# Splitting weight blocks on other engines: GpSimd's work in two grouped attentions handed to ScalarE and VectorE

## The reference

```python
# B: 32 query heads, 8 key heads, head width 128, 16 sequences of 64 tokens
q = (query @ Wq).reshape(nb, q_len, H, D).transpose(0, 2, 1, 3)
k = (key @ Wk).reshape(nb, q_len, KVH, D).transpose(0, 2, 1, 3)
v = (value @ Wv).reshape(nb, q_len, KVH, D).transpose(0, 2, 1, 3)
q = q * cos + _rotate_half(q) * sin
k = k * cos + _rotate_half(k) * sin
...
scores = jnp.where(mask == 0, -1e9, q @ k.T / sqrt(D))
x = softmax(scores) @ v          # k, v repeated for the 4 heads of a group
return x.reshape(nb, q_len, H * D) @ Wo
# D: the same without cos and sin, causal, query = key = value source
```

## Time and profile before

| | |
|---|---|
| time, median of 3 runs | 1838.44 us (1837.08 to 1838.74) |
| profiled execution, first to last instruction | 1832.8 us |
| PE busy | 1679.7 us, 92% |
| DVE busy | 1065.0 us, 58% |
| ACT busy | 603.0 us, 33% |
| POOL busy | 525.5 us, 29% |
| stretch of B's four passes of `turn` | 321.8 to 938.5 us |
| stretch of D's four passes of `turn` | 1037.9 to 1583.6 us |

### The profile page before, as it was taken

One profiled execution on the slowest core, in us unless ns is written; L12 is line 12 of the kernel. 1 busy time (PEld: TensorE's weight loads), 2 busy tenths in 40 slices (PEclk: granted clock), 3 DMA queues, 4 the chain that ended last, 5 costly groups with the idle time before them and its releaser, 6 DMA issues. The chain is left out here.

```text
span 1832.8 us, 24019 instructions
## 1 busy us (share of the span) xinstructions
PE 1679.7 (92%) x8910; PEld 1336.7 (73%) x8910; DVE 1065.0 (58%) x2105; ACT 603.0 (33%) x1199; POOL 525.5 (29%) x297
## 2 busy tenths in 40 slices
PE   8897879889998988989888999999999999888998
PEld 6665658667776866777677777777877877676866
DVE  3878775766676577566754245355265245517645
ACT  2564533223322323232243222222222222425541
POOL 4316123330323052120133323233053031432330
PEclk9998999899998989999999999999999999999999
DMA  4002011110111020000010111011021010112231
GB/s 178 14 18 81 25 35 46 47 35 12 36 35 46 1 70 24 23 24 24 23 42 27 57 35 47 12 57 46 0 69 46 0 46 24 47 33 61 71 91 46
DMA packets 26173, 75.78 MB, mean 41 GB/s; under 512 B 3904, under 2 KB 4640, under 8 KB 25824
## 3 DMA queue, kind: packets, MB, share of 16 engines
q1 hardware_dynamic: 25696, 73.42, 12.4%
q0 software_dynamic: 384, 1.05, 0.2%
HBM read 72.36 MB, written 2.10 MB: 41 GB/s over the span
## 5 line engine op out<-in xcount | busy, mean ns | idle before, releaser
L83 PE MATMUL bankA<-sb_xT,sb_Bwq 128*128 128x512 f32 x768 | 196.7, 407 | 0.0
L83 PE MATMUL bankY<-sb_Bwo,sb_BoT 128*128 128x512 f32 x768 | 195.9, 405 | 0.2 <-DVE sb_BoT L978 0.2
L83 PE MATMUL bankY<-sb_Dwo,sb_DoT 128*128 128x512 f32 x768 | 192.3, 399 | 2.0 <-POOL sb_Dwo L694 1.8
L83 PE MATMUL bankA<-sb_xT,sb_Dwq 128*128 128x512 f32 x768 | 189.9, 396 | 0.0
L83 PEld LDWEIGHTS bankY<-sb_Bwo,sb_BoT 128*128 128x128 f32 x768 | 142.8, 192 | 44.2 <-issue 15.0
L83 PEld LDWEIGHTS bankA<-sb_xT,sb_Bwq 128*128 128x128 f32 x768 | 147.4, 195 | 36.0 <-issue 2.7
L83 PEld LDWEIGHTS bankY<-sb_Dwo,sb_DoT 128*128 128x128 f32 x768 | 139.8, 188 | 44.0 <-issue 10.9
L83 PEld LDWEIGHTS bankA<-sb_xT,sb_Dwq 128*128 128x128 f32 x768 | 142.3, 188 | 33.9 <-issue 2.7
L919 DVE TENSOR_TENSOR sb_BqT<-bankA,sb_Btable 128x512 f32<-128x512 f32 x64 | 44.3, 692 | 183.5 <-ACT sb_Bsw L842 183.5
L78 POOL TENSOR_TENSOR sb_Bwo<-sb_raw,sb_zero 128x1024 fp32r<-128x1024 f32 x16 | 31.3, 1955 | 372.9 <-PE bankY L83 364.3
L78 POOL TENSOR_TENSOR sb_Dwo<-sb_raw,sb_zero 128x1024 fp32r<-128x1024 f32 x16 | 31.6, 1973 | 335.1 <-PE bankY L83 335.1
(11 more groups left out here) (253 smaller groups left out, 3406.3 us busy)
## 6 DMA issues: line engine op xcount, KB each, us to landing
sb_raw<-in_w_attn SPq DMA_DIRECT2D x80, 512.0 KB, 3.5
sb_raw<-in_q_gu SPq DMA_DIRECT2D x22, 256.0 KB, 2.7
sb_raw<-in_q_d SPq DMA_DIRECT2D x11, 256.0 KB, 2.6
sb_rawx<-in_xT SPq DMA_DIRECT2D x4, 512.0 KB, 8.0
sb_raw<-in_wqk SPq DMA_DIRECT2D x8, 256.0 KB, 2.6
sb_xtok<-in_x_tok SPq DMA_DIRECT2D x1, 2048.0 KB, 12.7
sb_raw<-in_ctxT SPq DMA_DIRECT2D x4, 512.0 KB, 3.8
sb_raw<-in_ctx_tok SPq DMA_DIRECT2D x4, 512.0 KB, 3.8
```

The costliest lines, as they stand in the source:

```text
L83: last = nc.tensor.matmul(out, lhs, rhs, start=start and i == 0, stop=stop and i == len(pairs) - 1)
```

## The change

All blocks of the passes of `turn`, 36 in each attention, are split elsewhere. The high part becomes a copy with ACT into the float32r buffer, the low part the same subtraction on DVE. POOL keeps the four blocks of `start` and the clearing of `kt`. The conditions for overwriting a buffer go along to ACT. In a `turn` the blocks have places in the slots: o0 and o2 in slots 0 and 8, on ACT ahead of `pt`, on DVE ahead of rotation, `front` and `back`; o1 and o3 in the same slots, on ACT after `pt`, on DVE after the low part of `oT`; the others at the end of the slot that `SPLIT_AT` names, on DVE after the low part of `oT` and ahead of a late `front`.

```diff
+    SPLIT_AT = {1: "q0", 3: "q1", 4: "k", 6: "v", 9: "q2", 11: "q3"}
...
                 @block.gpsimd
                 def _(pool):
-                    def split(part):
-                        for n, name in enumerate(part.blocks):
-                            if part.order is not START:
-                                if name == "o0":
-                                    pool.wait_ge(wo_used, part.it * 2 + 1)
...
-                            pool.wait_ge(w_raw[n % 2], (part.weights + n - n % 2) * 8 + 16)
-                            high_part(dst[name][0], raw[n % 2][:]).then_inc(w_high, 1)
-                            pool.wait_ge(w_high, part.weights + n + 1)
-                            nc.gpsimd.tensor_tensor(dst[name][1], raw[n % 2][:], f32(dst[name][0]), ALU.subtract).then_inc(w_low, 1)
-                            if part.order is START and name == "k":
-                                nc.gpsimd.memset(kt[:], 0.0).then_inc(padded, 1)
-                    run(pool, split, split)
+                    part = Part(first, START, START_BLOCKS)
+                    for n, name in enumerate(START_BLOCKS):
+                        pool.wait_ge(w_raw[n % 2], (part.weights + n - n % 2) * 8 + 16)
+                        high_part(dst[name][0], raw[n % 2][:]).then_inc(w_high, 1)
+                        pool.wait_ge(w_high, part.weights + n + 1)
+                        nc.gpsimd.tensor_tensor(dst[name][1], raw[n % 2][:], f32(dst[name][0]), ALU.subtract).then_inc(w_low, 1)
+                        if name == "k":
+                            nc.gpsimd.memset(kt[:], 0.0).then_inc(padded, 1)
...
+                    def weights_high(part, name):
+
+                        if name not in part.blocks:
+                            return
+                        n = part.blocks.index(name)
+                        if name in ("o0", "o2"):
+                            act.wait_ge(wo_used, part.it * 2 + (1 if name == "o0" else 2))
+                        elif name in ("o1", "o3"):
+                            act.wait_ge(y_done, part.it * SLOTS + (2 if name == "o1" else NT + 2))
+                        else:
+                            used = {"q0": ("Q", 5), "q1": ("Q", 7), "k": ("Q", 5), "v": ("Q", 5), "q2": ("Q", 13), "q3": ("Q", 15)}[name]
+                            act.wait_ge(a_ready, part.bank(used) + 1)
+                        act.wait_ge(w_raw[n % 2], (part.weights + n - n % 2) * 8 + 16)
+                        nc.scalar.activation(dst[name][0], raw[n % 2][:], ACT.Copy).then_inc(w_high, 1)
...
+                            if u % NT == 0:
+                                weights_high(part, "o2" if u else "o0")
                             act.wait_ge(t_ready, part.unit(u) + 1)
                             nc.scalar.activation(pt[u % 2][:], bankT[u % 2][:, 0:GROUP * S], ACT.Copy).then_inc(pt_done, 1)
+                            if u % NT == 0:
+                                weights_high(part, "o3" if u else "o1")
...
+                            if u in SPLIT_AT:
+                                weights_high(part, SPLIT_AT[u])
...
+                    def weights_low(part, name):
+
+                        if name not in part.blocks:
+                            return
+                        n = part.blocks.index(name)
+                        dve.wait_ge(w_high, part.weights + n + 1)
+                        nc.vector.tensor_tensor(dst[name][1], raw[n % 2][:], f32(dst[name][0]), ALU.subtract).then_inc(w_low, 1)
...
+                            if u % NT == 0:
+                                weights_low(part, "o2" if u else "o0")
                             in_turns(rotate(part, *banks) if rope and banks else None,
...
+                            if u % NT == 0:
+                                weights_low(part, "o3" if u else "o1")
+                            if u in SPLIT_AT:
+                                weights_low(part, SPLIT_AT[u])
                             if late(u):
                                 in_turns(scores)
```

## The result

The changed kernel takes 1766.84 us (median of 4 runs, 1765.95 to 1768.82) where the kernel before, run beside it, takes 1837.81 (1837.08 to 1838.74). The ratio is 0.9613, with a 95% interval of 0.9599 to 0.9626: 71 us faster. Forecast were 1764.5 us and a range of 1756 to 1788. The profiled execution took 1767.49 us beside a span of 1765.6, against 1832.8 of span before: 67.2 us of span.

What follows compares the result with a forecast made beforehand. In B's split slots, DVE instructions with two SBUF inputs stall beside POOL and PE waits. B gains 67.6 us (616.7 to 549.1), D 6.3, together 73.9: 1838.4 - 73.9 = 1764.5 us, range 1756 to 1788.

Steps and rivals of the forecast that it cites:

- the signs named: Profile afterwards: POOL empty in the turns, B's full passes 145 to 146 us at clock 1.00, D's 143 to 144.
- passes without the waits below: B's four passes: taken as D's 545.7 less its 7.4 us of waits, 538.3 us, products at full clock.
- rotation waits, twelve places: B's score products still wait for a rotation, 12 x 0.6 = 7.2 us of the earlier 23.4.
- slots 0 and 8, seven places: Splits of o0/o1 and o2/o3 in B, the tight place: 0.2 us booked for each of seven, 1.4 us.
- `pt` of the first slot: First slot of each attention: ACT's 1.06 us copy delays `pt(0)`, 1.1 us lost in B and 1.1 in D.
- waits for L978: Near the end of B, with no split there: 1.1 us of PE waits that stay.
- The clock: B's passes: granted clock returns to 1.00 as in D; otherwise 22.8 us would not come back, giving 1787.
- The first rival: Clock stays low in B because it keeps more waits than D: gain 51.1, time 1787 us; chance 0.06.
- The six other blocks: cost zero: q0 to q3, k, v at the ends of six slots: copy and low part covered, 1.4 us to spare.
- Low parts half exposed in B: Each of B's 36 blocks costs PE 0.6 us, 22 us go back: 1786 us; chance 0.11.
- The slower rival: Each block's copy and subtraction, 2.3 us, falls on PE's path: 1930 us; chance 0.03, with slower mixtures.
- No change: DVE's long instructions are not POOL's doing and the new work fits in idle time: 1838 us; chance 0.01.

Runs made afterwards that it cites:

- D alone: The change made in D only, B keeping its splits on POOL, against the kernel before: 1831.72 us, ratio 0.9963.
- the pair of useless loads: Changed kernel with POOL given two instructions per block on data nobody waits for: reading SBUF 1849.41 us, ratio 1.0054; only writing 1770.33, 0.9621.
- the rotation first: Changed kernel with late slots reordered: ACT's swap copies ahead of `pt`, DVE's rotation ahead of `back`; 1760.40 us, ratio 0.9583 to the kernel before.

## Why the prediction was right, and what was mis-sized

*What bounds the kernel, and by what.* Right, and shown: the waits of the earlier trace rows went with POOL's reads and came back with useless ones. The prices of the parts, 1.06 and 1.23, were measured as 1.06 and 1.22. Of the signs named, D's passes came a little better than 143 to 144 (142.5 to 143.4), and B's second and third, at 146.6 and 149.6, lie outside 145 to 146.

*B.* Here is the term that was off most. It said "B becomes 538.3 + 7.2 + 1.4 + 1.1 + 1.1 = 549.1", and it measured 554.6. Piece by piece:

| piece of B | booked | measured |
|---|---|---|
| passes without the waits below | 538.3 | 540.9 |
| rotation waits, twelve places | 7.2 | 7.0 |
| slots 0 and 8, seven places | 1.4 | 0 |
| `pt` of the first slot | 1.1 | 1.35 |
| waits for L978 (now L997) | 1.1 | 1.0 |
| waits behind the loop's jump | 0 | 4.3 |
| sum | 549.1 | 554.55 |

The waits are those of the list above, and for `pt` a single line of the order of time (below). The first row is D's passes without their wait for `pt` in the first slot, 537.9 - 0.8 = 537.1, and 3.8 us on top, by which PE is busy for longer in B's passes (534.9) than in D's (531.1). 3.3 of the 3.8 are in B's third pass: 145.79 against 142.5. This row isn't products at full clock alone, as the forecast had it: the 2.2 us of the last slot are in it in B and in D, before and after. The sum meets the 554.6 of the windows. Of the 5.5 us too many, 4.3 are the waits behind the jump. They were left out of the sum, though they were in the trace of before, 1.76 and 1.66 us at the same place. The sum took D's passes as its floor, and D's loop has no such wait.

*The clock.* "I let B's clock come back" was right for most of it: PE's busy time in B fell from 554.7 to 534.9, 19.8 of the 22.8 us. The first rival, a clock that stays low at 1787 us, is refuted: B's first two passes are at 1.00, with their rotation waits of 0.56 us. The third pass is not. The stretches behind the two loop jumps:

```profile
469.40:477.00 7.60, 5.44 (x31) 4.16 (x30) 5.63 (x12) 2.51 (x5) 0.00 (x0) 1.00 0.18 65
...
616.00:624.00 8.00, 5.88 (x21) 4.33 (x20) 5.96 (x12) 2.38 (x4) 0.00 (x0) 0.67 0.24 71
```

The same wait, 2.16 us at the second pass and 2.12 at the third, was followed by products at the full 2.4 GHz in the one and by a mean granted clock of 0.67 in the other, so part of that stretch ran at 1.2 GHz. The Trainium skill's rule on brief, frequent pauses ("TensorE: Matmul & The Clock Gate", section "A second HAM failure mode: psum-queue depth-cycling") isn't borne out by the pauses of 0.56 us here. What decides after one of 2.1 us these runs don't settle. Over the eleven profiles with the loop, the clock is below 1.00 in the 8 us behind 13 of the 22 waits, and length alone doesn't decide: it fell behind one of 1.94 us (B alone moved) and not behind one of 2.52 (low parts of o0 to o3 twice).

*D.* Booked 6.3, measured 7.8 in the windows and 7.9 for D alone. All waits on `back` and POOL went, and `pt(0)` cost this:

```profile
326.33 0.70 PE L791 MATMUL bankO<-sb_Bpt,sb_BV 64*128 64x256 f32 x4 [1.35 <-ACT sb_Bpt L879]
...
980.33 0.70 PE L791 MATMUL bankO<-sb_Dpt,sb_DV 64*128 64x256 f32 x4 [0.79 <-ACT sb_Dpt L879]
```

The 1.1 booked for each attention is the mean of the two, 1.35 in B and 0.79 in D. Before the change PE waited 0.41 us there in B, at 323.59, so the copy ahead of `pt(0)` added 0.94. D's passes without this wait came out 1.2 us below the floor of 538.3.

*The six other blocks: cost zero.* Right in the trace that was read. In a slot with q2:

```profile
543.26 0.42 ACT L842 ACTIVATE sb_Bsc<-sb_Bsc 128x256 f32<-128x256 f32 x1 [2.78 <-DVE sb_Bsc L948]
...
543.59 1.04 ACT L857 ACTIVATE sb_Bwq<-sb_raw 128x1024 fp32r<-128x1024 f32 x1
...
544.66 1.22 DVE L975 TENSOR_TENSOR sb_Bwq<-sb_raw,sb_Bwq 128x1024 fp32r<-128x1024 f32 x1 [0.50 <-ACT sb_Bwq L857]
...
547.39 0.69 DVE L928 TENSOR_TENSOR sb_BqT<-bankA,sb_Btable 128x512 f32<-128x512 f32 x1 [1.50 <-ACT sb_Bsw L830]
```

ACT does the copy behind its exponential, DVE the low part behind that, and DVE still stands idle for 1.50 us ahead of the rotation; the forecast had 1.4 to spare.

*The other rivals.* Low parts half exposed in B (1786) would have shown PE waiting for `Bwo` or `Bwq`; the changed kernel has no such wait. The doubled low parts of o0 to o3 show what it would look like. The slower rival is refuted for silent POOL, since a block costs PE nearly nothing. No change (POOL innocent) is refuted by the pair of useless loads.

*Span and time.* The sum took 1838.44 - 1832.8 = 5.6 us for what lies around the span. That was a misreading: in every execution on record with both numbers, of any kernel here, the time is 1.7 to 2.0 us above the span (1767.49 - 1765.6 = 1.9). By this the profiled execution before took an estimated 1834.6 us, 3.8 less than the median of the others. The spans differ by 67.2 us where 73.9 were booked: 5.5 too many in B, 1.5 too few in D, and 2.7 for the other stages, which came out longer. The forecast of the time is only 2.3 us off because the 5.6 was 3.7 too much and the profiled execution after was 0.6 above its median. That it came so near is in part luck; that it lies in the range isn't.

## What to carry to other kernels

Compare the longest and the median of each line, and where a few instructions of one form are three times the median, see what stands beside them in the order of time: here an engine with 29% of busy time cost TensorE some 60 us by what it did to VectorE. Moving such work to a busier engine pays if that engine has idle time in the slot, and the idle time ahead of its next instruction tells how much fits. Take span and time from the same execution: the difference between a profiled execution and the median of others isn't a cost around the span. When one stage serves as the floor for another, subtract its own waits and then go through the waits of the stage in question one by one, "issue" too.

## What the runs showed of the hardware

- POOL's instructions that read SBUF hold up DVE's with two SBUF inputs. Two per block that read, of 1.9 to 2.8 us, cost 79 us more than two memsets of 1.77 us, which only write: 1849.41 against 1770.33 us, the latter between nothing and 3.5 us above the changed kernel. DVE's lines with a PSUM operand or a single SBUF input were never longer for it (425 and 421 ns at most beside medians of 417 and 414). The hold-up goes both ways, since POOL's own instruction grew from 1.9 to 2.8 us.
- In a hardware loop with B's long body PE stood for 1.66 to 2.68 us a little behind the jump, in the middle of a product, in 22 of 22 jumps over eleven profiles. D's loop shows none, and with B written out there is none in the second and third pass. Why B's and not D's wasn't tried.
- A wait of 2.1 us left the granted clock at 1.00 once and was followed by 0.67 once, within one execution. Another execution, with the rotation first, had it the other way round: 0.79 behind the first such wait and 1.00 behind the second. Over all 22 the clock fell 13 times.
